# A graph convolution whose copied columns are collected over pairs of turns

## The chip, the cores and the metric

The kernel runs on one core of a Trainium2 chip. The metric is device time in microseconds (us) of one execution: the median of three runs of the kernel before is 3968.41 us, from 3967.84 to 3970.65.

## The reference

6250 nodes with 128 features and 206,250 edges sorted by destination (100,000 in both directions, and one loop per node). Two layers run one after the other, each as `x = x + layer(relu(layernorm(x)))`. The first is an attention layer with three edge types. The second, the only one that the change touches, is a convolution:

```
filters = silu(edge_attr @ fW1 + fb1) @ fW2 + fb2          # 50 attributes an edge
messages = (x[src] @ dW + db) * filters
aggregated = segment_sum(messages, dst)
return x + silu(aggregated @ uW1 + ub1) @ uW2 + ub2
```

## The kernel before

The first half of the time is the attention layer; at its end the product `x @ dW + db` of every node lies in a table in HBM (`table1`, a row per node), and the features themselves, transposed to one column per node, are read from `features` into SBUF (`by_node`, line 1561, a plane of `sums`).

**Units and turns.** The convolution goes through the edges in 269 units of 768 edges, six chunks of 128 (`CH`). Six units make a turn (`SL`); there are 45 turns (`TURNS`), the last of five units. Six gather buffers `xg[:, s]` belong to the six slots of a turn. The engines run their own instruction streams and meet at semaphores:

- GpSimd (POOL), `gather_units_beside`: for each unit one indirect DMA per chunk (line 63), which fetches 128 rows of `table1` into `xg`. A buffer is free when the product of the unit six back is done (`xg_free` is `s_msg`).
- TensorE (PE), `turn`: the first filter layer of a unit (line 1690, into `ps_h`), the second one of the unit before (line 1659, two banks `ps_f`), the sums by destination of the unit three back (line 1668), and once a turn a tile's update (1687, 1654).
- ScalarE (ACT): Silu of `ps_h` into `hid` (line 1609), and the transfers of the edge attributes (1592).
- VectorE (DVE), `turn` and `messages`: merge of a sum (line 1791), one-hot rows (1735), the bias sum on the filters (1773), then what `aside` puts in, then the product of filters and gathered rows (1783), which counts `s_msg` up. Reading the bases of a turn's windows into registers (`bases`, line 508) stands at the head of each turn.
- SyncE (SP), `load_beside`: index lists, finished tiles, and 64 rows a turn of one chunk by single row transfers (`Rows`).

**Columns.** Not every chunk is gathered. In turns 2 to 44 the last chunk of slots 1, 3 and 4 (of slot 4 half; the other half is SP's) is made from features in SBUF: VectorE and ScalarE each copy a share of the columns of its source nodes from `by_node` into `held`, one small copy a column (`collect`, lines 1748 and 1624, 4 bytes in each of 128 partitions); PE multiplies `held` by dW (`products`, line 1676); VectorE adds the bias and puts the rows into `xg` (`place`, line 1757). POOL leaves that chunk out. So a turn has 33 gathers. The addresses of the columns come from a list in SBUF (`columns`), read 16 at a time into registers (`READ`, `sources_at`, line 501). VectorE copies 24 columns a unit (144 a turn, 6192 in all), ScalarE 32, 32, 24, 32, 32, 24 (176 a turn, 7568 in all). In VectorE's order the copies stand behind the bias sum and the placement, ahead of the product.

**Loops.** VectorE's loop runs over turns 2 to 43 (`column_turns`), ScalarE's over 3 to 43 (`hinted_finishing_turns`), both with a hint for the branch back; PE's (`finishing_turns`) and POOL's have none. The turns ahead of a loop are written out.

Of the kernel before, what the change touches and what calls it, by code (L numbers as in the profile page):

```python
# [24 lines left out]
P = 128  # L25
CH = 6
UE = CH * P
SL = 6
NU = -(-E // (UE * SL)) * SL
TURNS = NU // SL  # L30
# [500 lines left out]
def hinted_finishing_turns(nc, engine, body):  # L531

    body(0, True, SL)
    for i in range(1, OPEN + 1):
        body(i, False, SL)
    with nc.Fori(OPEN + 1, SHUT, engines=[engine], hint_back_edge=True) as i:
        body(i, False, SL)
    body(SHUT, False, REST)


# [17 lines left out]
class Column:  # L558


    def __init__(self, to, placed, late, vector, scalar):
        self.to, self.placed, self.late, self.vector, self.scalar = to, placed, late, vector, scalar
        self.count = vector + scalar
# [3 lines left out]
COLUMNS = (Column(1, 5, False, 58, 70), Column(3, 1, True, 57, 71), Column(CARRY_SLOT, 3, True, 29, 35))  # L567
COLUMN_TURNS = TURNS - 2
TO = [column.to for column in COLUMNS]
ROWS = 64  # L570
ROW_TURNS = TURNS - 3
STORES = 48


class Share:


    def __init__(self, counts, held):
        self.counts, self.total = counts, sum(counts)
        self.held = [(m, e) for m, es in enumerate(held) for e in es]  # L580
        self.first, self.last = ({m: es[k] for m, es in enumerate(held)} for k in (0, -1))
        assert self.total == len(self.held)

    def start(self, s):
        return sum(self.counts[:s])

    def slot(self, s):
        return self.held[self.start(s):self.start(s + 1)]
# [6 lines left out]
def collects(i):  # L595
    return not (isinstance(i, int) and not 1 <= i <= COLUMN_TURNS)


def places(i, column):
    first = 2 if column.late else 1  # L600
    return not (isinstance(i, int) and not first <= i < first + COLUMN_TURNS)


def takes(i):
    return not (isinstance(i, int) and i < 2)


def column_rows(rows):

    turn = np.arange(2, TURNS)  # L610
    chunk = [rows[(turn * SL + to) * CH + CH - 1] for to in TO]
    return np.concatenate([chunk[m][:, e:e + 1] for share in (SCALAR, VECTOR) for m, e in share.held], 1)
# [7 lines left out]
def column_at(r, i, m):  # L620

    return r * COLUMN_TURNS * len(COLUMNS) + (i - 1) * len(COLUMNS) + m
# [27 lines left out]
def landed_beside(r, i, s):  # L650

    if s in TO:
# [5 lines left out]
def column_turns(nc, engine, body):  # L658

    body(0, True, SL)  # L660
    body(1, False, SL)
    with nc.Fori(2, TURNS - 1, engines=[engine], hint_back_edge=True) as i:
        body(i, False, SL)
    body(TURNS - 1, False, REST)
# [153 lines left out]
def gather_units_beside(pool, passes, table, xg, idx, idx_in, gathered, xg_free, pool_turn):  # L818

    with pool.Fori(0, passes) as r:  # L820
        def turn(i, first, count):
            for s in range(count):
                if s % LOAD == 0:
                    pool.wait_ge(idx_in[s // LOAD], 16 * (r * TURNS + i + 1))
                pool.wait_ge(xg_free, r * UNITS + (XS if first else i * SL + s + 1))  # L825
                pool.sem_inc(pool_turn, 1)
                for c in range(CH - 1 if s in TO and takes(i) else chunks_of(i, s)):
                    k = s % LOAD * CH + c
                    gather(pool, xg[:, s, c, :], table, idx[s // LOAD][:, k:k + 1], gathered[s])

        turn(0, True, SL)
        turn(1, False, SL)
        with pool.Fori(2, TURNS - 1) as i:
            turn(i, False, SL)
        turn(TURNS - 1, False, REST)


class Rows:
# [9 lines left out]
    def landed(self, eng, r, i, s):  # L848
        if s == CARRY_SLOT and takes(i) and not (isinstance(i, int) and i == TURNS - 1):
# [13 lines left out]
def load_beside(nc, sp, a, h, idx, idx_in, gathered, landed, rows, xg, xg_free, ahead, beside, listed):  # L863

    def read(r, i, v, count=SL):

        s = min(v * LOAD + LOAD, count) - 1
        sp.wait_ge(gathered[s], landed_beside(r, i, s))
# [635 lines left out]
def convolution_edges(nc, h, a, acc, update, table, features, planes, sent, sources, project, y, out):  # L1504

    with ExitStack() as ctx:
# [23 lines left out]
        drawn = sb("drawn", [COLUMN_TURNS, SCALAR.total + VECTOR.total], i32)  # L1530
        columns = sb("columns", [33, COLUMN_TURNS * SCALAR.total], i32)
        by_row = [drawn[:, 0:SCALAR.total], drawn[:, SCALAR.total:]]
        held = sb("held", [P, len(COLUMNS), P])
# [10 lines left out]
        def _(sp):  # L1544
# [6 lines left out]
            sp.dma_start(drawn[:, :], a["column_rows"][:, :]).then_inc(lists_in, 16)  # L1551

            sp.wait_ge(scaled, 2)
            for k, share in enumerate((SCALAR, VECTOR)):
                sp.dma_start(columns[32 * k:32 * k + 1, 0:COLUMN_TURNS * share.total].rearrange("o (t c) -> o t c", c=share.total), by_row[k]).then_inc(table_in, 16)

            def tables(r):

                sp.wait_ge(project.last_turned, 16)
                sp.wait_ge(s_column, r * COLUMN_TURNS * len(COLUMNS) + len(COLUMNS))  # L1560
# [25 lines left out]
        def _(act):  # L1586
            act.wait_ge(w_in, 64)
            act.wait_ge(update.loaded, 64)
            with act.Fori(0, pass_count(act, h)) as r:
# [5 lines left out]
                def turn(i, first, count):  # L1595
                    for s in range(count):
# [6 lines left out]
                        if opens(i) and s == 1:  # L1603
                            k = r * DONE + i - OPEN
                            act.wait_ge(t_u, k + 1)
                            if not (isinstance(i, int) and i == OPEN):
                                act.wait_ge(t_v, k)
# [3 lines left out]
                        if collects(i):  # L1611
                            collect(i, s)

                def collect(i, s):

                    if s == 0:
                        act.wait_ge(table_in, 16 * (r + 3))
                        act.sem_inc(begun, 1)
                    starts = sources_at(nc, mybir.EngineType.Activation, columns[0:1, :], (i - 1) * SCALAR.total + SCALAR.start(s), SCALAR.counts[s])
                    for (m, k), start in zip(SCALAR.slot(s), starts):  # L1620
                        if k == SCALAR.first[m]:
                            act.wait_ge(s_column, column_at(r, i, m) + 1)
                            act.sem_inc(begun, 1)
                        one = nc.scalar.copy(held_bytes[:, 4 * (m * P + k):4 * (m * P + k) + 4], by_byte[:, bass.ds(start, 4)])  # L1624
                        if k == SCALAR.last[m]:
                            one.then_inc(s_other, 1)
                hinted_finishing_turns(nc, mybir.EngineType.Activation, turn)
# [10 lines left out]
        def _(pe):  # L1638
# [4 lines left out]
            with pe.Fori(0, pass_count(pe, h)) as r:  # L1643
                def filters(n, s, fresh, i=None, at=None):
# [10 lines left out]
                    for m, column in enumerate(COLUMNS):  # L1655
                        if at is not None and at[1] == column.placed and places(at[0], column):
                            products(at[0] - 1 if column.late else at[0], m, b)
# [13 lines left out]
                def products(i, m, b):  # L1671

                    k = column_at(r, i, m)
                    pe.wait_ge(s_half, k + 1)
                    pe.wait_ge(s_other, k + 1)
# [238 lines left out]
```

## Time and profile before

| | |
|---|---|
| runs, median (lowest to highest) | 3968.41 us (3967.84 to 3970.65) |
| profiled execution, its own time | 3967.15 us |
| its span, first to last instruction | 3965.3 us |
| mean granted TensorE clock | 0.624 |
| gathers of the convolution (line 63) | 1485, 947 ns each, busy 1406.5 us |
| column copies on ScalarE (line 1624) | 7568, busy 796.0 us, idle before them 325.4 us |
| column copies on VectorE (line 1748) | 6192, busy 688.5 us, idle before them 258.9 us |
| message products on VectorE (line 1783) | 269, 957 ns each, idle before them 151.2 us |

A group's busy time is the time in which at least one of its instructions ran; idle is the time in which its engine stood still just ahead of them, with what ended most of it. "issue" means that the profile shows nothing it waited for: the engine's sequencer was reading registers, computing addresses or fetching. DVE is VectorE, ACT ScalarE, POOL GpSimd, SP SyncE; a q behind the name is its sequencer or queue. Granted clock 1.0 is 2.4 GHz, 0.5 is 1.2 GHz.

### The profile page before, as it was taken

The page shows a single profiled execution, that of the slowest core. Times are in us where ns is not written, and L with a number is a line of the kernel's source. Part 1 is how long each engine was busy: PE and PEld are TensorE (multiplying, and loading weights), DVE is VectorE, ACT ScalarE, POOL GpSimd, SP SyncE. Part 2 cuts the span into 40 slices and gives each one's busy share as a digit, 9 for nine tenths or more (in the row PEclk, how much of TensorE's full clock was granted, in tenths as well). Part 3 has the DMA queues.
Part 4 walks back from the last instruction along what each step waited for, and adds up shares of the span by engine and source line. Part 5 has one row for each costly group of instructions (what it writes and reads, how often), then busy time and mean ns, then how long its engine had stood idle before and what let it go on. Part 6 is the DMA issues. An engine that isn't in the chain of part 4 may idle for free. (4 is left out here: it accounts for less than half of the span.)

```text
span 3965.3 us, 95687 instructions
## 1 busy us (share of the span) xinstructions
PE 3326.2 (84%) x14263; PEld 2589.5 (65%) x14264; DVE 3095.7 (78%) x11649; ACT 2162.5 (55%) x10967; POOL 2948.0 (74%) x3109
## 2 busy tenths in 40 slices
PE   5788888888888888888876898889888889999898
PEld 3566666666666666666655776767676767777676
DVE  7888888888888888888875777777777777777775
ACT  5455555555555555555543665556555565655563
POOL 6777777777777777777757777777777777777776
PEclk7555555555555555555557777777777777767767
DMA  4222222222222222222225332333233332333232
GB/s 127 57 62 61 62 64 62 62 63 63 63 61 63 62 63 62 62 63 63 60 48 145 83 81 76 80 81 79 77 80 80 81 80 76 81 80 81 75 81 68
DMA packets 193989, 289.07 MB, mean 73 GB/s; under 512 B 85379, under 2 KB 138047, under 8 KB 189036
## 3 DMA queue, kind: packets, MB, share of 16 engines
q0 software_dynamic: 98464, 205.11, 21.8%
q1 hardware_dynamic: 90364, 40.65, 4.1%
q10 hardware_dynamic: 4840, 40.55, 3.4%
q14 instruction: 306, 2.51, 0.2%
q8 instruction: 15, 0.25, 0.0%
HBM read 267.39 MB, written 15.70 MB: 71 GB/s over the span
## 5 line engine op out<-in xcount | busy, mean ns | idle before, releaser
L63 POOL DMA_INDIRECT ae_xg<-table,ae_idx x1592 | 1502.3, 944 | 491.6 <-issue 487.4
L63 POOL DMA_INDIRECT ce_xg<-table,ce_idx x1485 | 1406.5, 947 | 458.8 <-issue 443.6
L1624 ACT COPY ce_held<-sums 128x4 uint8 x7568 | 796.0, 189 | 325.4 <-issue 311.3
L1748 DVE COPY ce_held<-sums 128x4 uint8 x6192 | 688.5, 199 | 258.9 <-issue 243.0
L1150 PE MATMUL ae_ps_k<-ae_xg,ae_e 128*96 128x129 f32 x3224 | 880.8, 431 | 0.0
L1150 PEld LDWEIGHTS ae_ps_k<-ae_xg,ae_e 128*96 128x96 f32 x3224 | 688.6, 276 | 126.5 <-issue 117.0
L1659 PE MATMUL ce_ring<-ce_fw,ce_hid 128*128 128x128 f32 x3228 | 610.2, 362 | 61.1 <-DVE ce_msg L1783 60.8
L1659 PEld LDWEIGHTS ce_ring<-ce_fw,ce_hid 128*128 128x128 f32 x3228 | 564.6, 269 | 138.5 <-DVE ce_msg L1783 90.7
L1690 PE MATMUL ce_ps_h<-ce_ea,ce_fw 50*128 50x384 f32 x1076 | 532.9, 626 | 45.8 <-DMA ce_ea<-in_edge_attr 29.2
L1062 ACT ACTIVATE ae_upper<-ring 128x576 f32<-128x576 f32 x269 | 174.9, 650 | 671.5 <-DVE ring L1327 671.5
L1668 PEld LDWEIGHTS ce_ring<-ce_hot,ce_msg 128*128 128x128 f32 x3224 | 487.0, 236 | 5.2 <-DVE ce_msg L1783 5.2
L1609 ACT ACTIVATE ce_hid<-ce_ps_h,ce_fb 128x768 f32<-128x768 f32 x269 | 241.8, 899 | 445.9 <-issue 279.0
L1668 PE MATMUL ce_ring<-ce_hot,ce_msg 128*128 128x32 f32 x3224 | 476.1, 305 | 2.8 <-DVE sums L1791 2.8
L1070 ACT ACTIVATE ae_off<-cst,plan 128x96 bf16<-128x96 f32 x1614 | 454.1, 363 | 5.0 <-DVE plan L491 5.0
L1783 DVE TENSOR_TENSOR ce_msg<-ce_ring,ce_xg 128x768 f32<-128x768 f32 x269 | 257.5, 957 | 151.2 <-DMA ce_xg<-table,ce_idx 146.1
L1198 PE MATMUL ring<-ae_rise,cst 64*128 64x192 f32 x538 | 270.2, 604 | 83.4 <-DVE ae_rise L1350 80.4
L1165 PE MATMUL ae_ps_tz<-cst,ae_high 128*96 128x128 f32 x269 | 120.2, 447 | 255.1 <-DVE ae_high L1337 255.1
L1690 PEld LDWEIGHTS ce_ps_h<-ce_ea,ce_fw 50*128 50x128 f32 x1076 | 219.4, 226 | 167.5 <-issue 65.7
L1327 DVE TENSOR_TENSOR ring<-ring,ae_xg 128x576 f32<-128x576 f32 x269 | 205.9, 766 | 129.7 <-DMA ae_xg<-table,ae_idx 126.0
L1337 DVE TENSOR_REDUCE ae_high<-ae_e 128x96 f32<-128x576 f32 x269 | 304.6, 1132 | 0.0
L1773 DVE TENSOR_TENSOR ce_ring<-ce_ring,ce_fb 128x768 f32<-128x768 f32 x269 | 257.7, 958 | 58.1 <-PE ce_ring L1659 57.9
L1165 PEld LDWEIGHTS ae_ps_tz<-cst,ae_high 128*96 128x96 f32 x269 | 41.8, 156 | 319.6 <-DVE ae_high L1337 319.6
(193 smaller groups left out, 3804.8 us busy)
## 6 DMA issues: line engine op xcount, KB each, us to landing
ce_stage<-table SPq DMA_DIRECT2D x2688, 0.5 KB
ae_stage<-table SPq DMA_DIRECT2D x2560, 0.5 KB
ce_ea<-in_edge_attr ACTq DMA_DIRECT2D x88, 450.0 KB
ae_xg<-table,ae_idx POOLq DMA_INDIRECT x1592
ce_xg<-table,ce_idx POOLq DMA_INDIRECT x1485
sums<-in_x SPq DMA_DIRECT2D x7, 448.0 KB, 4.5
sums<-features SPq DMA_DIRECT2D x1, 3136.0 KB
table<-sums SPq DMA_DIRECT2D x6, 462.0 KB, 3.6
```

The source lines that it names most:

```text
L63: eng.indirect_dma_start(out=out, out_offset=None, in_=table[:, :], in_offset=bass.IndirectOffsetOnAxis(ap=idx, axis=0)).then_inc(done, 16)
L1070: last = nc.scalar.activation(off[:, s % 2, c, :], h.iota, ACT.Square, bias=keys[:, c:c + 1], scale=STEP)
L1150: last = nc.tensor.matmul(ps_k[0:KEYS, 0:D + 1], by_chunk[s % 3][:, c, :], xg[:, s % XS, c, 0:D + 1], start=(c == 0), stop=(c == count - 1))
L1198: nc.tensor.matmul(ps_m[s % 2][:, 0:2 * KEYS], h.raised_by[0:64, :], rise[:, :, :].rearrange("p a k -> p (a k)"), start=True, stop=True).t ...
L1337: nc.vector.tensor_reduce(out=high[:, :], in_=by_chunk[s % 3].rearrange("p c k -> p k c"), op=ALU.max, axis=AX.X).then_inc(s_high, 1)
L1624: one = nc.scalar.copy(held_bytes[:, 4 * (m * P + k):4 * (m * P + k) + 4], by_byte[:, bass.ds(start, 4)])
L1659: last = nc.tensor.matmul(ps_f[b][:, c * D:(c + 1) * D], hid[:, b, c * P:(c + 1) * P], fw2[:, :], start=True, stop=True)
L1668: last = nc.tensor.matmul(ps_a[s % 2][:, 0:W], msg[:, s % 3, c, :], hot[:, s % 3, c, :], start=(c == 0), stop=(c == count - 1))
L1690: last = nc.tensor.matmul(ps_h[:, k * 512:k * 512 + H], fw1[:, :], ea[:, s // LOAD, q:q + H], start=True, stop=True)
L1748: one = nc.vector.tensor_copy(held_bytes[:, 4 * (m * P + k):4 * (m * P + k) + 4], by_byte[:, bass.ds(start, 4)])
L1773: nc.vector.tensor_tensor(filt, filt, fb2[:, :].unsqueeze(1).to_broadcast([P, CH, D]), ALU.add).then_inc(s_bias, 1)
L1783: nc.vector.tensor_tensor(msg[:, s % 3, :, :], filt, xg[:, s % XS, :, :], ALU.mult).then_inc(s_msg, 1)
```

## The change

All convolution loops run over pairs of turns: pair k is turns 2k+1 and 2k+2, k from 0 to 21; pairs 1 to 20 are the loop, the rest is written out. VectorE's and ScalarE's loops keep the hint and get a set position of their first instruction (`head_slot` 8 and 100). A pair collects seven chunks in its twelve units. Each engine copies 32 columns a unit, half of every chunk: 384 a pair, 8224 in all (the last pair collects three chunks, in five units). The seventh chunk is the last one of slot 0 of the odd turns 3 to 43; POOL leaves it out too. `held` has four buffers in place of three, used in rotation. The lists are laid out by pair and reach SBUF by way of `msg`; VectorE and ScalarE wait for them ahead of their loops. A column is placed three units after its last copies. In VectorE's order nothing else moves.

```diff
-COLUMNS = (Column(1, 5, False, 58, 70), Column(3, 1, True, 57, 71), Column(CARRY_SLOT, 3, True, 29, 35))
-COLUMN_TURNS = TURNS - 2
+PAIRS = TURNS // 2
+PIECE, HELD = 32, 4
+COLUMNS = (Column(1, 1, (0, 1), P), Column(3, 1, (2, 3), P), Column(CARRY_SLOT, 1, (4,), P - ROWS), Column(0, 2, (5, 6), P),
+           Column(1, 2, (7, 8), P), Column(3, 2, (9, 10), P), Column(CARRY_SLOT, 2, (11,), P - ROWS))
...
+        self.to, self.ahead, self.slots, self.count = to, ahead, slots, count
+        self.late, self.placed = divmod(slots[-1] + 3, 2 * SL)
...
-SCALAR = Share([32, 32, 24] * 2, [range(c.vector, c.count) for c in COLUMNS])
-VECTOR = Share([24] * SL, [range(c.vector) for c in COLUMNS])
...
+def since(m):
+    return HELD if m >= HELD else len(COLUMNS) - (m + HELD if m + HELD < len(COLUMNS) else m) + m
...
+def served(i, k, p, s):
+    if isinstance(i, int) and i < 2 + (s == 0):
+        return None
+    return next(((m, column.ahead - 1) for m, column in enumerate(COLUMNS) if column.to == s and column.ahead == 2 - p), None)
...
+def paired_turns(pairs, body):
+    body(0, True, SL, None, 0)
+    for i in (1, 2):
+        body(i, False, SL, 0, i - 1)
+    with pairs as k:
+        for p in range(2):
+            body(2 * k + 1 + p, False, SL, k, p)
+    body(TURNS - 2, False, SL, PAIRS - 1, 0)
+    body(TURNS - 1, False, REST, PAIRS - 1, 1)
+
+def hinted_pairs(nc, engine, slot):
+    return nc.Fori(1, PAIRS - 1, engines=[engine], hint_back_edge=True, head_slot={engine: slot})
...
-                for c in range(CH - 1 if s in TO and takes(i) else chunks_of(i, s)):
+                for c in range(chunks_of(i, s) if served(i, k, p, s) is None else CH - 1):
...
+            dve.wait_ge(lists_in, 64)
...
-                    if s == 0:
-                        dve.wait_ge(table_in, 16 * (r + 3))
-                        dve.sem_inc(begun, 1)
-                    starts = sources_at(nc, mybir.EngineType.DVE, columns[32:33, :], (i - 1) * VECTOR.total + VECTOR.start(s), VECTOR.counts[s])
-                    for (m, k), start in zip(VECTOR.slot(s), starts):
-                        if k == VECTOR.first[m]:
-                            dve.wait_ge(s_column, column_at(r, i, m) + 1)
-                            dve.sem_inc(begun, 1)
-                        one = nc.vector.tensor_copy(held_bytes[:, 4 * (m * P + k):4 * (m * P + k) + 4], by_byte[:, bass.ds(start, 4)])
-                        if k == VECTOR.last[m]:
-                            one.then_inc(s_half, 1)
+                    m, first = column_in(q)
+                    if not COLUMNS[m].here(k):
+                        return
+                    if q == COLUMNS[m].slots[0]:
+                        dve.wait_ge(s_column, column_at(r, k, m) + 1 + len(COLUMNS) - since(m))
+                        dve.sem_inc(begun, 1)
+                    if q == 0:
+                        dve.wait_ge(table_in, 16 * (r + 1))
+                        dve.sem_inc(begun, 1)
+                    at = 4 * (m % HELD * P + 0 * COLUMNS[m].count // 2 + first)
+                    starts = sources_at(nc, mybir.EngineType.DVE, columns[0:1, :], k * pair_columns + q * PIECE, PIECE)
+                    for start in starts:
+                        last = nc.vector.tensor_copy(held_bytes[:, at:at + 4], by_byte[:, bass.ds(start, 4)])
+                        at += 4
+                    if q == COLUMNS[m].slots[-1]:
+                        last.then_inc(s_half, 1)
...
-                hinted_finishing_turns(nc, mybir.EngineType.Activation, turn)
+                paired_turns(hinted_pairs(nc, mybir.EngineType.Activation, 100), turn)
...
-                column_turns(nc, mybir.EngineType.DVE, turn)
+                paired_turns(hinted_pairs(nc, mybir.EngineType.DVE, 8), turn)
```

## Rows read from the trace of the kernel before

**Rows 1.** The page, part 1: each engine's busy us, share, instructions.
```profile
PE 3326.2 (84%) x14263; PEld 2589.5 (65%) x14264; DVE 3095.7 (78%) x11649; ACT 2162.5 (55%) x10967; POOL 2948.0 (74%) x3109
```

**Rows 2.** Windows: busy us by engine, granted clock, DMA share, GB/s.
```profile
2222.00:3915.00 1693.00, 1512.21 (x7301) 1206.28 (x7300) 1234.48 (x7094) 986.22 (x7476) 1280.46 (x1354) 0.74 0.31 79
```

**Rows 3.** The chain of waits of that stretch, shares by line.
```profile
by line: POOL ce_xg L63 56.1%; issue 22.0%; DMA ce_xg<-table,ce_idx 4.9%; PE ce_ring L1659 3.4%; PE ce_ps_h L1690 3.1%; PE ce_ring L1668 2.3%; DVE ce_held L1748 1.3%; DVEq L501 1.0%; DVE ce_msg L1783 0.8%; POOLq L825 0.6%; DMA ce_idx<-in_sr
```

**Rows 4.** POOL's group in that stretch: busy, mean ns, idle, releasers.
```profile
L63 POOL DMA_INDIRECT ce_xg<-table,ce_idx x1354 | 1281.3, 946 | 412.8 <-issue 404.9 <-DVE ce_msg L1783 6.7 <-DMA ce_idx<-in_src 1.2
```

**Rows 5.** VectorE's waits in that stretch: us in total, times, longest us.
```profile
DVE ce_msg L1783 <- DMA ce_xg<-table,ce_idx: 124.6, 69, 3.9
...
DVE ce_ring L1773 <- PE ce_ring L1659: 30.9, 27, 2.4
DVE ce_done L1811 <- DMA out_x<-ce_done: 4.1, 8, 0.8
```

**Rows 6.** VectorE's timeline, two turns: start, us, instruction, idle before.
```profile
2184.80 0.96 DVE L1783 TENSOR_TENSOR ce_msg<-ce_ring,ce_xg 128x768 f32<-128x768 f32 x1
2186.28 0.19 DVE L1791 TENSOR_TENSOR sums<-sums,ce_ring 128x32 f32 x1 [0.53 <-issue]
...
2194.08 0.28 DVE L1757 TENSOR_TENSOR ce_xg<-ce_ring,pj_parts 128x128 f32<-128x128 f32 x1
2194.27 1.71 DVE L1748 COPY ce_held<-sums 128x4 uint8 x16
2196.65 0.92 DVE L1748 COPY ce_held<-sums 128x4 uint8 x8 [0.67 <-issue]
...
2221.80 0.96 DVE L1783 TENSOR_TENSOR ce_msg<-ce_ring,ce_xg 128x768 f32<-128x768 f32 x1
...
3007.67 0.19 DVE L1791 TENSOR_TENSOR sums<-sums,ce_ring 128x32 f32 x1 [0.74 <-issue]
...
3009.62 1.89 DVE L1748 COPY ce_held<-sums 128x4 uint8 x16 [0.56 <-issue]
```

**Rows 7.** Two lines on VectorE: count, ns min/median/max.
```profile
L501 DVEq TENSOR_LOAD <-ce_columns x516: 594/852/1126, 2148.8 to 3912.5; - x172
...
L1748 DVEq ALU_OP  x5904: 40/40/45, 2226.0 to 3913.8; - x197
L1748 DVE COPY ce_held<-sums x5904: 150/172/431, 2226.1 to 3913.9; 128x4 uint8 x197
```

**Rows 8.** ScalarE: its timeline, and its largest wait in the stretch.
```profile
3003.17 0.90 ACT L1609 ACTIVATE ce_hid<-ce_ps_h,ce_fb 128x768 f32<-128x768 f32 x1 [3.32 <-issue]
...
3009.44 0.89 ACT L1609 ACTIVATE ce_hid<-ce_ps_h,ce_fb 128x768 f32<-128x768 f32 x1
...
3012.96 1.80 ACT L1624 COPY ce_held<-sums 128x4 uint8 x16 [0.92 <-issue]
...
3019.84 0.76 ACT L1624 COPY ce_held<-sums 128x4 uint8 x7 [0.48 <-issue]
...
ACT ce_hid L1609 <- issue: 272.5, 95, 5.2
```

**Rows 9.** PE's timeline at 1.2 GHz, filters to filters.
```profile
2859.64 2.93 PE L1659 MATMUL ce_ring<-ce_fw,ce_hid 128*128 128x128 f32 x12
...
2868.34 1.06 PE L1659 MATMUL ce_ring<-ce_fw,ce_hid 128*128 128x128 f32 x4
```

**Rows 10.** The head: VectorE's timeline, its first bias sum.
```profile
2123.05 0.97 DVE L1773 TENSOR_TENSOR ce_ring<-ce_ring,ce_fb 128x768 f32<-128x768 f32 x1 [9.37 <-PE ce_ring L1659]
```

**Rows 11.** VectorE's timeline: products at the ends of three stretches.
```profile
2143.45 0.96 DVE L1783 TENSOR_TENSOR ce_msg<-ce_ring,ce_xg 128x768 f32<-128x768 f32 x1 [3.26 <-DMA ce_xg<-table,ce_idx]
...
3876.23 0.96 DVE L1783 TENSOR_TENSOR ce_msg<-ce_ring,ce_xg 128x768 f32<-128x768 f32 x1
...
3914.81 0.96 DVE L1783 TENSOR_TENSOR ce_msg<-ce_ring,ce_xg 128x768 f32<-128x768 f32 x1 [0.70 <-DMA ce_xg<-table,ce_idx]
...
3953.55 0.96 DVE L1783 TENSOR_TENSOR ce_msg<-ce_ring,ce_xg 128x768 f32<-128x768 f32 x1 [4.77 <-DMA ce_xg<-table,ce_idx]
```

More of the change, by code:

```diff
@@ L528, in finishing_turns @@
     body(SHUT, False, REST)
[L531 to L538, printed above, removed]
 def opens(i):
@@ L558, with __init__, pair, here @@
 class Column:
-    def __init__(self, to, placed, late, vector, scalar):
-        self.to, self.placed, self.late, self.vector, self.scalar = to, placed, late, vector, scalar
-        self.count = vector + scalar
+    def __init__(self, to, ahead, slots, count):
+        self.to, self.ahead, self.slots, self.count = to, ahead, slots, count
+        self.late, self.placed = divmod(slots[-1] + 3, 2 * SL)
+    def pair(self, k):
+        return k - self.late
+    def here(self, k):
+        return not (isinstance(k, int) and not 0 <= k < (PAIRS if self.ahead == 1 else PAIRS - 1))
@@ L572 @@
 STORES = 48
[L575 to L588, printed above, removed]
-SCALAR = Share([32, 32, 24] * 2, [range(c.vector, c.count) for c in COLUMNS])
@@ L592, with column_in @@
-VECTOR = Share([24] * SL, [range(c.vector) for c in COLUMNS])
[L595 to L605, printed above, removed]
-def column_rows(rows):
-    turn = np.arange(2, TURNS)
-    chunk = [rows[(turn * SL + to) * CH + CH - 1] for to in TO]
-    return np.concatenate([chunk[m][:, e:e + 1] for share in (SCALAR, VECTOR) for m, e in share.held], 1)
+def column_in(q):
+    return next((m, PIECE * column.slots.index(q)) for m, column in enumerate(COLUMNS) if q in column.slots)
@@ new lines, in since @@
+def since(m):
[4 more added lines that the diff above has]
+    return next(((m, column.ahead - 1) for m, column in enumerate(COLUMNS) if column.to == s and column.ahead == 2 - p), None)
+def column_rows(rows):
+    pair = np.arange(PAIRS)
+    padded = np.concatenate([rows, np.zeros((SL * CH, P), rows.dtype)])
+    chunk = [padded[((2 * pair + 1 + column.ahead) * SL + column.to) * CH + CH - 1] for column in COLUMNS]
+    parts = []
+    for half in range(2):
+        for q in range(2 * SL):
+            m, e = column_in(q)
+            first = half * COLUMNS[m].count // 2 + e
+            parts.append(chunk[m][:, first:first + PIECE])
+    return np.concatenate(parts, 1)
@@ L820, in gather_units_beside, with turn @@
     with pool.Fori(0, passes) as r:
-        def turn(i, first, count):
+        def turn(i, first, count, k, p):
             for s in range(count):
@@ L826, in turn @@
                 pool.sem_inc(pool_turn, 1)
-                for c in range(CH - 1 if s in TO and takes(i) else chunks_of(i, s)):
[L828 to L835, printed above, removed]
+                for c in range(chunks_of(i, s) if served(i, k, p, s) is None else CH - 1):
+                    j = s % LOAD * CH + c
+                    gather(pool, xg[:, s, c, :], table, idx[s // LOAD][:, j:j + 1], gathered[s])
+        paired_turns(pool.Fori(1, PAIRS - 1), turn)
 class Rows:
@@ L848, in landed @@
     def landed(self, eng, r, i, s):
-        if s == CARRY_SLOT and takes(i) and not (isinstance(i, int) and i == TURNS - 1):
+        if s == CARRY_SLOT and not (isinstance(i, int) and (i < 2 or i == TURNS - 1)):
             eng.wait_ge(self.carried, 16 * (r * ROW_TURNS + i - 1))
@@ L1655, in filters @@
                     for m, column in enumerate(COLUMNS):
-                        if at is not None and at[1] == column.placed and places(at[0], column):
-                            products(at[0] - 1 if column.late else at[0], m, b)
+                        if at is not None and at[0] is not None and at[1] == column.placed and column.here(column.pair(at[0])):
+                            products(column.pair(at[0]), m, b)
                     for c in range(CH):
@@ L1762, in aside @@
                         return
-                    i, s = at
+                    k, q = at
                     for m, column in enumerate(COLUMNS):
-                        if s == column.placed and places(i, column):
-                            place(i - 1 if column.late else i, m, (s - 1) % SL % 2)
-                    if collects(i):
-                        collect(i, s)
-                def messages(n, s, i, at=None):
+                        if q == column.placed and column.here(column.pair(k)):
+                            place(column.pair(k), m, (q - 1) % SL % 2)
```

131 lines of the change are left out of this document (68 added, 63 removed).

## The prediction

> **What bounds the kernel now.** I began with the page's busy shares [rows 1]. They single out no engine: PE is busy for 84%, VectorE (DVE) for 78%, GpSimd (POOL) for 74%. The change touches only the second half, the convolution, so I cut out its steady stretch, 2222 to 3915 us, in which VectorE goes 41 times round its loop: 1693.0 / 41 = 41.29 us a turn [rows 2]. The chain of waits of that stretch is POOL's gather for 56.1%, with 22.0% "issue" [rows 3]. POOL's group says what that issue is: its gathers are busy for 1281.3 us with 412.8 idle between them, of which 404.9 wait for nothing, the step from one gather to the next [rows 4]. So (1281.3 + 412.8) / 1354 = 1.251 us a gather, 33 a turn, 41.29 us: POOL alone sets the turn.
>
> Next comes how much air the others have. VectorE's waits for other engines and transfers in the stretch are 124.6 + 30.9 + 4.1 [rows 5] and 3.9 in two smaller groups, 163.5 us, 3.99 a turn. The rest of its turn, 37.30 us, is its own: instructions, and "issue" gaps in which its sequencer reads sources into registers or computes addresses. A turn early in the stretch, when POOL is still ahead, confirms it: from one message product at 2184.80 to the one six units on at 2221.80 there are 37.0 us, without an outside wait [rows 6]. So the slack under POOL is 4.0 us a turn, and the question is what the change adds to VectorE.
>
> **POOL's part.** Per pair of turns one more chunk (slot 0 of the odd turn) comes from the table in SBUF, 21 gathers fewer in all: 65 a pair, or 81.3 us, 40.66 a turn. If POOL stays the bound this is worth 21 x 1.251 = 26.3 us. That is all the change can gain there.
>
> **VectorE's part.** It copied 144 columns a turn (24 a unit: a read of 16 registers and 16 copies, a read of 8 and 8 copies). Now it copies 32 a unit, 192 a turn: the second read is of 16 too, with 16 copies behind it.
> - Copies: a batch of 8 spans 0.92 us and one of 16 spans 1.71 us [rows 6], so 8 more cost 0.79; by batches that start on an idle engine (1.89 less 0.92 [rows 6]) 0.97. With 0.17 for one copy [rows 7], (0.92 - 0.17) / 7 = 0.107 us a copy. I take 0.86 us a unit, 5.14 a turn.
> - Register reads: half are of 16 and half of 8, so minimum and maximum are the two sizes: 0.594 and 1.126 us, the median 0.852 lying between the halves [rows 7]. I take 1.10 for the long one. The second read is bare: between the 16 and the 8 copies the engine idles 0.66 us each time [rows 6]. ScalarE, which has both sizes, idles 0.48 us ahead of 8 copies and 0.92 ahead of 16 [rows 8]. So the gap grows by 0.44 (ScalarE) to 0.53 us; I take 0.50 a unit, 3.0 a turn. The first read lies under the bias sum (0.96 us) before as after.
> - Placements: 7 a pair in place of 6, at 0.28 us [rows 6] and two waits: 0.2 a turn. Waits and semaphore steps at a column's start: 3.5 a turn instead of 3, but at a unit's head, not between copies: 0.
>
> Sum: 5.14 + 3.0 + 0.2 = 8.3 us a turn against a slack of 4.0. Nothing covers it: copies, reads, bias sum, product and merge are one engine's one queue. VectorE's turn becomes 37.3 + 8.3 = 45.6 us (45.3 from the 37.0), above POOL's 40.66. I take 45.5. Below, the cheapest reading is 36.5 + 0.79 x 6 + 0.44 x 6 = 43.9 (36.5 estimated as 37.0 less the 0.5 us before the merge [rows 6]); above, it is 37.3 + 0.97 x 6 + 0.53 x 6 + 0.3 = 46.6.
>
> **ScalarE's part.** 176 columns a turn become 192, two of its six units growing from 24 to 32. A unit of 32 takes from 3009.44 to 3014.76, 5.3 us [rows 8], six of them 32, and the stall at its loop's back edge (3.32 us [rows 8]), now once a pair, 1.7 more. The issue of two attribute transfers and one small activation a turn would have to cost 11 us before ScalarE reached 45.5: no cost. The fourth held buffer and `since` make each collection wait for the product four columns back, placed at least one slot earlier in PE's order: no cost.
>
> **PE's part.** Half a product more a turn (0.5 to 0.8 us). At a clock of 1.2 GHz a unit takes 8.70 us (2859.64 to 2868.34) [rows 9]; over the stretch PE is busy for 1512.2 / 246 = 6.15 us a unit, at a granted clock of 0.74, so about half of the time at each level [rows 2]. A unit will be 7.58 us on VectorE, so PE falls behind 1.1 us a unit while slow and catches up when fast. It can: filters are two banks deep, so they can be ready some 4.6 us (7.6 less 2.93) before VectorE wants them. With less slack (6.88 a unit) it made VectorE wait 30.9 us in 1693 [rows 5]. I add nothing.
>
> **The head.** VectorE now waits, before it builds the keys, for the two transfers of the column lists, which SP issues as soon as they are scaled. I estimate up to 5 us for them, half of what follows: behind the keys VectorE idles 9.37 us for the first filters (2123.05) [rows 10]. Cost 0, at most 3. The lists in `msg` are dead before the first product.
>
> **The tail.** Turn 44 copies nothing. Before, POOL holds it: 3914.81 to 3953.55, 38.7 us [rows 11]. Now POOL has these gathers nearly done when VectorE arrives, and the six units run at PE's pace, 6.15 each: 36.9, a gain of 1.8 (from 0 to 10). Turn 43 has five units of 32 columns and one of none: 45.5 less 4.7 (twice 1.71, and 1.2 for the read and the gap between), 40.8 against 38.6 (3876.23 to 3914.81), +2.2.
>
> **The sum**, on the profiled run's own 3967.15 us (its span is 3965.3): the copies' stretch runs from 2143.45 to 3876.23 [rows 11], 42 turns and 1732.8 us. Its first turn (41.3 us) has 4 us of start-up waits that stay: 41.3 + 8.3 = 49.6. The other 41 x 45.5 = 1865.5. Together 1915.1, +182.3; with tail and turn 43, +182.7. The changed kernel takes 3967.15 + 182.7 = **4150 us**; the median of the runs, 3968.41, is 1.3 above the profiled run, too little to move it.
>
> **A rule against the change: the back edge.** VectorE goes round its loop almost free: ahead of the first merge of a turn it idles 0.53 us in a turn that stands outside the loop (2186.28) and 0.74 where it has just gone round (3007.67) [rows 6]. ScalarE, with a slightly longer body, stands 3.32 us "issue" at each turn's head, and over the stretch its activations have 272.5 us of such idle [rows 8]. A body of a pair has on VectorE more than twice the instructions. If VectorE then stalls as ScalarE does, that is 20 times 3.3 us = 66 us. The Trainium skill (Runtime: NRT & Kernel Launch, section "Instruction fetch mechanics") gives the reason: an engine holds two pages of 256 instructions, and a branch back to a page it no longer holds waits for a fetch. By that rule a body over 512 instructions cannot stay, and the new one has 768 in its copies alone, an address and a copy for each column; whether the prefetch hint and the new head slots (8 and 100) hide the fetch, no trace here shows.
>
> **Rivals.**
> - VectorE stalls at the back edge: 4150 + 66 = 4216 us. For: ScalarE's stall with the same hint. Against: VectorE's own back edge, hinted too, costs 0.2 us [rows 6]. 14%.
> - POOL stays the bound and the change is faster: VectorE's new work would have to fit in 4.0 us a turn. It decides where the addition falls below 4.0: over half of the 8.3 would have to vanish. 3967 - 26 = 3941 us. 5%.
> - The longer reads and their gap cost nothing (hidden behind queued copies): 37.3 + 5.3 = 42.6 a turn, 41 x 42.6 + 46.6 = 1793, +60: 4028 us. Against it the bare 0.66. 6%.
> - PE's slow phases are not absorbed: half the units at 8.7 and half at 7.6 give 48.9 us a turn, 41 x 3.4 more: 4150 + 139 = 4289 us. For: the waits for filters. Against: the two banks. 6%.
> - My forecast, VectorE the bound at 45.5 us: 69%, own range 4100 to 4185.
>
> **Numbers.** Range 4090 to 4230: it holds the forecast with its bounds and the back edge, and leaves out 4028, 3941 and 4289 (17%) with a little of the tails. A measurement of this kernel can tell 0.2% (8 us) from no change. Faster 5%; the same 2% (slack and addition happening to cancel with POOL's gain); slower 93%.
>
> **What would show it.** Right: the changed profile has VectorE's message products every 7.5 us, copies in 16 + 16 with a gap near 1.15 us, 8224 copies on each engine, hardly a wait of VectorE for gathers, and new gaps on POOL, released by VectorE's product, of some 4.8 us a turn. Long register reads and no short ones. PE's granted clock falls little. Wrong: POOL's gathers still without a break (then my price of copies or reads is wrong), gaps over 2 us on VectorE once a pair (back edge), or VectorE's wait for filters above 2 us a turn.

## The result: 4.7% slower, and the profile after

The changed kernel takes 4158.09 us (median of 4 runs, 4153.78 to 4160.27), the kernel before 3969.53 on the same chip (4 runs). The ratio is 1.0473 (95% interval 1.0455 to 1.0491), +188.6 us; the forecast was 4150. The profiled run after took 4160.1 us with a span of 4158.3.

First the page's busy shares (the row that answers to [rows 1]).

```profile
PE 3471.5 (83%) x14305; PEld 2730.8 (66%) x14306; DVE 3316.9 (80%) x13702; ACT 2208.0 (53%) x11623; POOL 2926.0 (70%) x3088
```

VectorE (DVE) has 221 us more work, 2053 instructions more; POOL has 21 instructions and 22 us less. Now the second half's steady stretch, 2327 to 4074 us, 19 rounds of the new loop (each a pair of turns), as windows; the second row is the tail.

```profile
2327.00:4074.00 1747.00, 1528.56 (x6803) 1240.19 (x6802) 1344.91 (x8418) 958.90 (x7562) 1173.28 (x1243) 0.68 0.27 71
4074.00:4158.00 84.00, 76.95 (x366) 59.85 (x365) 48.25 (x223) 23.77 (x145) 36.36 (x39) 0.74 0.20 50
```

1747.0 / 38 = 45.97 us a turn, 91.95 a pair, where [rows 2] gave 41.29 a turn. The granted clock of TensorE is 0.68 against 0.74. What now sets the turn is read from two views of that stretch: the chain of waits by line,

```profile
by line: issue 26.4%; DVE ce_held L1755 24.9%; DVEq L501 21.5%; DVE ce_ring L1780 6.4%; PE ce_ring L1662 2.8%; DVEq L508 2.3%; DVE ce_hot L1738 2.1%; PE ce_ps_h L1692 2.1%; PE ce_ring L1671 1.9%; DVEq L1755 1.4%; DVE sums L1797 1.3%; DVE ce
```

and the waits (us in total, times, longest):

```profile
POOL ce_xg L63 <- issue: 355.8, 1116, 2.4
DVE ce_held L1755 <- issue: 333.8, 377, 1.3
...
POOL ce_xg L63 <- DVE ce_msg L1789: 218.2, 127, 3.3
...
DVE sums L1797 <- issue: 38.9, 38, 1.8
...
DVE ce_msg L1789 <- issue: 9.4, 19, 0.5
...
DVE ce_hot L1738 <- issue: 6.0, 19, 0.3
DVE ce_ring L1780 <- PE ce_ring L1662: 1.3, 4, 0.4
```

POOL's gather, 56.1% of the chain in [rows 3], is gone from it. VectorE's copies (L1755) and its sequencer's reads of their sources (L501) stand in its place. VectorE waited 163.5 us for others before [rows 5]; now the last row is the only one of that kind, 1.3 us. POOL waits instead, for VectorE's message product, 218.2 us, 5.7 a turn where I had said some 4.8. The timeline of VectorE shows one pair's beginning, with start, duration (us), instruction and the idle time before it:

```profile
3064.02 0.96 DVE L1789 TENSOR_TENSOR ce_msg<-ce_ring,ce_xg 128x768 f32<-128x768 f32 x1
3066.70 0.19 DVE L1797 TENSOR_TENSOR sums<-sums,ce_ring 128x32 f32 x1 [1.72 <-issue]
...
3068.60 1.93 DVE L1755 COPY ce_held<-sums 128x4 uint8 x16 [0.52 <-issue]
3071.53 1.77 DVE L1755 COPY ce_held<-sums 128x4 uint8 x16 [1.00 <-issue]
3073.30 0.96 DVE L1789 TENSOR_TENSOR ce_msg<-ce_ring,ce_xg 128x768 f32<-128x768 f32 x1
...
3078.88 1.77 DVE L1755 COPY ce_held<-sums 128x4 uint8 x16 [1.12 <-issue]
3080.76 0.96 DVE L1789 TENSOR_TENSOR ce_msg<-ce_ring,ce_xg 128x768 f32<-128x768 f32 x1
```

Where [rows 6] had 16 + 8 copies with 0.66 us between, there are 16 + 16 with 1.00 to 1.12. The line of the reads, and the copies' group of the page (each of the two engines makes 8224):

```profile
L501 DVEq TENSOR_LOAD <-ce_columns x514: 1095/1101/1305, 2151.5 to 4110.3; - x172
...
L1755 DVE COPY ce_held<-sums 128x4 uint8 x8224 | 909.9, 202 | 379.5 <-issue 376.7
```

No short read is left (minimum 594 ns in [rows 7]). The ends of the stretches, as VectorE's products (they answer to [rows 11]):

```profile
2147.59 0.96 DVE L1789 TENSOR_TENSOR ce_msg<-ce_ring,ce_xg 128x768 f32<-128x768 f32 x1
...
4073.79 0.96 DVE L1789 TENSOR_TENSOR ce_msg<-ce_ring,ce_xg 128x768 f32<-128x768 f32 x1
...
4113.35 0.96 DVE L1789 TENSOR_TENSOR ce_msg<-ce_ring,ce_xg 128x768 f32<-128x768 f32 x1
```

| stretch (us) | before | forecast | after |
|---|---|---|---|
| 42 turns with copies | 1732.8 | 1915.1 | 1926.2 |
| turn 43 | 38.6 | 40.8 | 39.6 |
| last turn and what follows it (to the span's end) | 50.5 | 48.7 | 44.9 |
| up to the first of these products | 2143.4 | 2143.4 | 2147.6 |

The differences are +193.4, +1.0, -5.5 and +4.1: 193.0, as the spans have it (4158.3 less 3965.3).

### The profile page after: what moved, and what is told of

The parts are those of the page before. It is cut to its first block and busy times, and to the rows that moved or that the text cites. A ratio compares the mean times of both kernels' runs of the same rounds, so it can differ in the third digit from the quotient of the medians.

```text
span 4158.3 us, 100937 instructions
## 1 busy us (share of the span) xinstructions
PE 3471.5 (83%) x14305; PEld 2730.8 (66%) x14306; DVE 3316.9 (80%) x13702; ACT 2208.0 (53%) x11623; POOL 2926.0 (70%) x3088
## 5 line engine op out<-in xcount | busy, mean ns | idle before, releaser
L63 POOL DMA_INDIRECT ce_xg<-table,ce_idx x1464 | 1384.4, 946 | 653.4 <-issue 419.8
L1755 DVE COPY ce_held<-sums 128x4 uint8 x8224 | 909.9, 202 | 379.5 <-issue 376.7
L1625 ACT COPY ce_held<-sums 128x4 uint8 x8224 | 841.7, 189 | 376.7 <-issue 359.1
L1145 PEld LDWEIGHTS ae_ps_k<-ae_xg,ae_e 128*96 128x96 f32 x3224 | 688.7, 277 | 126.4 <-issue 117.0
L1662 PE MATMUL ce_ring<-ce_fw,ce_hid 128*128 128x128 f32 x3228 | 685.3, 394 | 81.6 <-DVE ce_msg L1789 81.1
L1662 PEld LDWEIGHTS ce_ring<-ce_fw,ce_hid 128*128 128x128 f32 x3228 | 637.3, 299 | 164.0 <-DVE ce_msg L1789 125.0
L1692 PE MATMUL ce_ps_h<-ce_ea,ce_fw 50*128 50x384 f32 x1076 | 541.9, 635 | 27.7 <-DMA ce_ea<-in_edge_attr 24.5
L1671 PEld LDWEIGHTS ce_ring<-ce_hot,ce_msg 128*128 128x128 f32 x3224 | 536.3, 256 | 1.0 <-issue 0.7
L1671 PE MATMUL ce_ring<-ce_hot,ce_msg 128*128 128x32 f32 x3224 | 519.9, 321 | 0.0
L1160 PEld LDWEIGHTS ae_ps_tz<-cst,ae_high 128*96 128x96 f32 x269 | 41.9, 156 | 318.1 <-DVE ae_high L1332 318.1
```

What stands on the lines that cost most here:

```text
L63: eng.indirect_dma_start(out=out, out_offset=None, in_=table[:, :], in_offset=bass.IndirectOffsetOnAxis(ap=idx, axis=0)).then_inc(done, 16)
L1145: last = nc.tensor.matmul(ps_k[0:KEYS, 0:D + 1], by_chunk[s % 3][:, c, :], xg[:, s % XS, c, 0:D + 1], start=(c == 0), stop=(c == count - 1))
L1625: last = nc.scalar.copy(held_bytes[:, at:at + 4], by_byte[:, bass.ds(start, 4)])
L1662: last = nc.tensor.matmul(ps_f[b][:, c * D:(c + 1) * D], hid[:, b, c * P:(c + 1) * P], fw2[:, :], start=True, stop=True)
L1671: last = nc.tensor.matmul(ps_a[s % 2][:, 0:W], msg[:, s % 3, c, :], hot[:, s % 3, c, :], start=(c == 0), stop=(c == count - 1))
L1692: last = nc.tensor.matmul(ps_h[:, j * 512:j * 512 + H], fw1[:, :], ea[:, s // LOAD, q:q + H], start=True, stop=True)
```

## Experiments

The theory is the forecast's: VectorE's own queue sets the turn, and of what the change added 5.1 us a turn is copies and 3.0 is the longer bare read. The rivals are a stall at the pair loop's back edge, a POOL that stays the bound, and PE's slow phases. Each edit is against the changed kernel; ratios are against the kernel before, run on the same chip.

**Parts of the added work taken away from VectorE.** In e1 and e8 its second read is of 8 registers, in e2 it makes 24 copies, in e3 both. None of the four computes the whole convolution: in e1 and e8 most columns in the second half of a piece of 32 come from a wrong source, in e2 and e3 eight of 32 stay zero.

```diff
 # e1_reads_24: read 24 sources, copy 32; the last 8 sources serve two copies each
-starts = sources_at(..., k * pair_columns + q * PIECE, PIECE)
-for start in starts:
+starts = sources_at(..., k * pair_columns + q * PIECE, 24)
+for start in twice(starts):        # from the 17th on each source twice
```

> VectorE reads 16 + 8 addresses a unit and still makes 32 copies (its last 8 copies take an address a second time). VectorE bound with bare reads: 0.50 us a unit less, 3.0 of 45.9 a turn, 42 turns, 126 us off the changed kernel's 4158: 4032 us. If the longer reads hide behind queued copies: 4158 us, no change.

3948.74 us (3945.0 to 3960.77), ratio 0.996 (0.9926 to 0.9994): 83 us below what was expected. VectorE's timeline tells why.

```profile
3064.13 1.72 DVE L1763 COPY ce_held<-sums 128x4 uint8 x16
3066.51 1.23 DVE L1763 COPY ce_held<-sums 128x4 uint8 x16 [0.66 <-issue]
```

The second batch of 16 spans 1.23 us, not 1.77. By the line's rows there are 6168 address computations for 8224 copies:

```profile
L1763 DVE COPY ce_held<-sums x8224: 150/172/429, 2147.8 to 3896.4; 128x4 uint8 x196
L1763 DVEq ALU_OP  x6168: 40/40/47, 2147.8 to 3896.1; - x199
```

Two copies from the same source share one computation, so the edit took away eight of these per unit as well, and POOL was the bound again (it waited 2.7 us for VectorE's products in 1500). The mended twin has distinct sources:

```diff
 # e8_reads_24_distinct, in twice()
-            yield start
+            yield start + 4
```

> As e1, but each of VectorE's 32 copies has an address computation of its own again (the last 8 take an address read before, plus 4 bytes, so these columns are another node's). If e1 gained twice because copies that share an address skip that computation (0.071 us instead of 0.107, 16 of them a unit, 3.3 us a turn) and the shorter read gave 3.0: now only the read's part remains, 4158 - 126 = 4032 us. If the read alone gave e1's whole gain: 3949 us again.

4032.08 us (4029.34 to 4034.82), ratio 1.0159 (1.0139 to 1.0179). As expected: with 8224 computations the batch is back at 1.77 us, behind the same short gap.

```profile
L1763 DVEq ALU_OP  x8224: 40/40/47, 2150.9 to 3986.5; - x196
```

```profile
3070.70 1.77 DVE L1763 COPY ce_held<-sums 128x4 uint8 x16 [0.66 <-issue]
```

The eight registers more per read are worth 4158.1 - 4032.1 = 126 us, 126 / 42 = 3.0 us a turn, the term as priced. Next the copies, and both.

```diff
 # e2_copies_24: 32 sources read, the last 8 not copied (held is zeroed once, ahead)
 for e, start in enumerate(starts):
+    if e >= 24:
+        continue
 # e3_both_24: 24 read, 24 copied
```

> VectorE reads all 32 addresses a unit and copies only the first 24 (8 columns of each piece stay zero). VectorE bound at 0.107 us a copy: 5.1 us a turn less, 40.8, beside POOL's 40.7: 3950 to 3980 us. If VectorE's copies were not what sets the turn (PE's slow phases or ScalarE instead): above 4100 us.

> VectorE reads 24 addresses and copies 24 (the other 8 columns of each piece stay zero), all else as in the changed kernel. VectorE falls to 37.9 us a turn, POOL with its 21 gathers fewer is the bound again at 40.66: 3935 to 3955 us, 26 below the kernel before. If POOL's saved gathers are worth nothing (another engine as late as POOL): 3968 or more.

e2: 3940.81 us (3938.87 to 3946.94), ratio 0.9935 (0.9912 to 0.9957), 9 us below the range expected. e3: 3941.67 (3941.03 to 3942.75), 0.9934 (0.9911 to 0.9956). Both are where POOL would be the bound (3941). In e3, between 2400 and 3900 us, POOL's waits are

```profile
POOL ce_xg L63 <- issue: 360.9, 1184, 0.3
POOL ce_xg L63 <- DVE ce_msg L1790: 4.3, 14, 0.3
```

so its gathers run without a break, 1.25 us each, 65 a pair. Two things follow: the form with pairs costs nothing by itself and brings the gain of 21 fewer gathers (27 us, 26.3 worked out); and what eats them is VectorE's work. In e2 the long gap stays (3076.77, ahead of 8 copies), and still the time is POOL's: without the copies VectorE's turn is at most POOL's 40.7, so by the turn the copies were worth at least 45.97 - 40.7 = 5.3 us. Their own busy time gives the size. The rows are one batch of e2 and e2's group of copies over the whole run:

```profile
3076.77 0.92 DVE L1758 COPY ce_held<-sums 128x4 uint8 x8 [1.07 <-issue]
```

```profile
L1758 DVE COPY ce_held<-sums 128x4 uint8 x6168 | 688.7, 200 | 395.3 <-issue 391.3
```

The changed kernel's group has 909.9 us (above), both in 257 units: (909.9 - 688.7) / 257 = 0.86 us a unit, 5.2 a turn, where 5.14 was forecast.

**The back edge.**

```diff
 # e4_no_hint: VectorE's loop alone loses the hint of its branch
-hint_back_edge=True
+hint_back_edge=engine != mybir.EngineType.DVE
```

> VectorE's loop without the hint for its branch back, its position kept. If the hint is what keeps the fetch of the loop's first block out of the way: some 3.3 us a pair more, 20 pairs, 4158 + 66 = 4224 us. If the block is fetched in time anyway: 4158 us; if every pair pays already, no change either.

4194.52 us (4193.83 to 4195.21), ratio 1.0566 (1.0536 to 1.0597): 36 us above the changed kernel. Once a pair, ahead of the merge of its first turn, VectorE idles 4.04 us in place of 1.72:

```profile
3087.66 0.19 DVE L1797 TENSOR_TENSOR sums<-sums,ce_ring 128x32 f32 x1 [4.04 <-issue]
```

In the waits of 2400 to 3900 us the merge's idle is this without the hint, and this in the changed kernel:

```profile
DVE sums L1797 <- issue: 69.4, 32, 4.2
```

```profile
DVE sums L1797 <- issue: 34.4, 33, 1.7
```

So the stall exists and the hint covers it here; unhinted it is 4.04 - 1.72 = 2.3 us a pair by the timeline, (69.4 - 34.4) / 16.3 pairs = 2.1 by the waits, not the 3.3 that the rival took from ScalarE. The run's own 36 us, 1.8 a pair, are about half of the 66 expected.

**Six chunks a pair in place of seven**: the added chunk, and so two units' copies, dropped; POOL gathers it again (41.3 us a turn).

```diff
 # e5_six_chunks (and what column_in() and landed_beside() need for it)
-COLUMNS = (..., Column(CARRY_SLOT, 1, (4,), P - ROWS), Column(0, 2, (5, 6), P),
+COLUMNS = (..., Column(CARRY_SLOT, 1, (4,), P - ROWS),
 # e9_six_chunks: e5, and held buffers given so that no collection waits for a late product
+BUFFER, SINCE = (0, 1, 2, 3, 1, 2), (6, 3, 3, 6, 3, 3)
```

> Loops over pairs, but without the seventh chunk (slot 0 of the odd turn is gathered again; slots 5 and 6 of a pair collect nothing): 320 columns a pair on each engine. VectorE bound theory: VectorE falls by 64 x 0.17 = 11 us a pair to 81.1, POOL sets 82.6 as before: 3968 to 3990 us. If the form of the loop (longer body, instruction fetch, one common pace of the engines) is what costs: above 4050 us.

4112.44 us (4095.67 to 4116.63), ratio 1.0349 (1.0324 to 1.0374), a miss by over 120. ScalarE idled up to 10.2 us ahead of its copies, which I took for waits for a held buffer, so I mended the buffers:

> As e5, with the buffers of held given out so that no collection waits for a product that PE issues only in the next pair. If e5's time was that new wait (ScalarE stood 8 us a pair in it), it goes and VectorE's own 84 us a pair is the bound: 3975 to 4000 us. If the form of the loop costs: 4110 us again.

4125.99 us (4120.35 to 4145.25), ratio 1.0412 (1.0384 to 1.0439): a second miss. The longest idle ahead of ScalarE's copies is down to 1.1 us and the time no better, so that wait was not the cause. VectorE's timeline in e9, over the two units that now copy nothing:

```profile
3064.66 0.96 DVE L1789 TENSOR_TENSOR ce_msg<-ce_ring,ce_xg 128x768 f32<-128x768 f32 x1
...
3067.14 0.96 DVE L1789 TENSOR_TENSOR ce_msg<-ce_ring,ce_xg 128x768 f32<-128x768 f32 x1 [0.29 <-DVE ce_ring L1780]
...
3070.35 0.96 DVE L1789 TENSOR_TENSOR ce_msg<-ce_ring,ce_xg 128x768 f32<-128x768 f32 x1
...
3078.52 0.97 DVE L1780 TENSOR_TENSOR ce_ring<-ce_ring,ce_fb 128x768 f32<-128x768 f32 x1 [6.26 <-PE ce_ring L1662]
```

These units take 2.5 and 3.2 us, then VectorE stands 6.26 us for the next filters. PE's timeline shows why they are late:

```profile
3056.34 1.61 PE L1662 MATMUL ce_ring<-ce_fw,ce_hid 128*128 128x128 f32 x12 [1.53 <-DVE ce_msg L1789]
...
3065.89 0.77 PE L1678 MATMUL ce_ring<-pj_dw,ce_held 128*128 128x128 f32 x2 [5.20 <-DVE ce_msg L1789]
3066.45 2.77 PE L1662 MATMUL ce_ring<-ce_fw,ce_hid 128*128 128x128 f32 x12
```

PE had stood 5.20 us until VectorE's product gave it a bank, and the twelve matmuls of the filters took 2.77 us behind that wait where they took 1.61 before it. It needs 6.15 us a unit on the mean [rows 2] and 8.70 at 1.2 GHz [rows 9] and is at most two banks ahead, so a mean over the pair says nothing: VectorE cannot save up what the empty units leave. The waits for filters are 95.8 us in 1500, 1.3 in the changed kernel; over the 1900 us of the turns with copies that is some 120 us, the size of the miss.

Both times lie where "the form of the loop costs" would have put them. That reading is out by e3, which has the same form and loses nothing, and by the idle ahead of the merges in e9, 34.9 us in 1500 where the changed kernel has 34.4. No run here has more than two banks, so that a third would help is not shown.

**Columns moved from VectorE to ScalarE**, with the whole result. 28 to 36:

```diff
 # e6_28_36 (each engine's list at its own stride, the small lists moved to a third row)
-PIECE, HELD = 32, 4
+PIECES_OF, HELD = (28, 36), 4
 # e7_28_36_bases: e6, and VectorE reads the bases of 12 units once a pair, not 6 twice
+elif p == 0: base = pair_bases[:] = bases(..., i * SL - back, 2 * SL)
 # e10_28_36_at104: e6, and the loop's head at another slot
-paired_turns(hinted_pairs(nc, mybir.EngineType.DVE, 8), turn)
+paired_turns(hinted_pairs(nc, mybir.EngineType.DVE, 104), turn)
```

> The changed kernel with its columns shared out anew: VectorE 28 a unit, ScalarE 36; all seven chunks, the reference's whole output. VectorE bound theory: 4 x 0.17 us a unit less on VectorE, 41.9 us a turn, ScalarE at some 41: 4158 - 172 = 3986 us, up to 4010 where the two get in each other's way. If total copying and not VectorE's share sets the turn: 4100 us or more.

> As the one before, and the bases of both turns of a pair are read by VectorE in one read of 12 registers at the pair's head instead of two of 6. VectorE bound theory: the gap ahead of a merge goes once a pair, some 0.5 us a turn if VectorE is still the bound: 20 us below the one before, about 3970. If ScalarE or POOL is the bound there: no change from it.

> As e6, with the first instruction of VectorE's loop at position 104 in place of 8, so that the branch back stands where it stands in the changed kernel (104 + 893 = 997 = 8 + 989). If the 2.2 us that e6 stands at each back edge come from that position: 1.7 us a pair less, 4037 - 35 = 4002 us. If they come from the body's length or its contents: 4037 us.

e6: 4036.57 us (4029.81 to 4058.65), ratio 1.0158 (1.0141 to 1.0175), 27 us above the range expected. e7: 4046.81 (4042.62 to 4051.0), 1.0198 (1.0181 to 1.0215), a miss: it was to gain 20 and lost 10. e10: 4017.01 (3988.58 to 4021.47), 1.0097 (1.006 to 1.0134), the best that computes everything, and still behind the kernel before; it is 20 us below e6 where 35 were expected (37 by the two profiled runs, 4058.65 and 4021.47). The merge's idle tells them apart, in the waits of 2400 to 3900 us of e6, of e7 and of e10:

```profile
DVE sums L1797 <- issue: 68.4, 34, 3.9
```

```profile
DVE sums L1799 <- issue: 92.9, 18, 5.6
```

```profile
PE ce_ps_h L1692 <- ACT ce_hid L1606: 63.2, 47, 3.6
...
DVE sums L1797 <- issue: 32.3, 33, 1.8
...
DVE ce_ring L1780 <- PE ce_ring L1662: 12.6, 16, 1.2
...
DVE sums L1797 <- PE ce_ring L1671: 3.5, 2, 1.8
```

Taking copies out of VectorE's loop made its body shorter, and with the head at the same slot the branch came to lie elsewhere: the stall returned in full although the hint stood (68.4 against 34.4; unhinted 69.4). Four copies fewer in 12 units, each a copy and an address computation, are 96 instructions; moving the head by 96 slots puts the branch back to where the changed kernel has it, and took the stall away: 32.3. e1 bears this out: its loop is shorter by 96 address computations with the head at slot 8, so by this count its branch lies where e6's does, though it has all 32 copies. Its merges' idle in the same stretch, hidden there under POOL, is

```profile
DVE sums L1805 <- issue: 65.2, 33, 3.8
```

e8, with these computations back, has 36.4.

In e7 the long read of the bases stands bare right behind that stall. The rows are the read of 6 bases at the head of a pair in the changed kernel, and e7's read of 12:

```profile
L508 DVEq TENSOR_LOAD <-base_i x1: 1422/1422/1422, 3064.9 to 3064.9; - x1
```

```profile
L508 DVEq TENSOR_LOAD <-base_i x1: 2742/2742/2742, 3014.4 to 3014.4; - x1
```

That is 1.3 us more a pair, against the 0.33 us of idle ahead of the second turn's merge that it saves.

VectorE is still the bound in e10: it waits 12.6 + 3.5 us for PE in 1500, and its 212 bias sums in that stretch make 42.5 us a turn, above POOL's 40.66. The 41.9 expected of VectorE's own turn held (42.5 less 0.5 of waits). PE's 63.2 us for ScalarE's hidden layer reach VectorE only as far as those 16 us.

27 to 37:

```diff
 # e11_27_37: as e10
+PIECES_OF, HELD = (27, 37), 4
 # e12_27_37_aligned: every unit's list begins at a multiple of 16 bytes
+PIECES_OF, STRIDES, HELD = (27, 37), (28, 40), 4
```

> As e10, with 27 columns a unit on VectorE and 37 on ScalarE. VectorE bound theory: 12 x 0.17 = 2 us a pair less on VectorE, 82.2, with ScalarE and POOL beside it at 81 to 82: 3955 to 3985 us. If ScalarE is already the bound at 36: slower than e10.

5105.5 us (5102.55 to 5107.77), ratio 1.2861 (1.2839 to 1.2882): a miss by over 1100. The line of the reads, on both engines of e11:

```profile
L501 ACTq TENSOR_LOAD <-ce_columns x771: 549/1229/3674, 2147.9 to 5058.7; - x193
L501 DVEq TENSOR_LOAD <-ce_columns x514: 1110/2515/3732, 2150.3 to 5054.2; - x172
```

A read takes up to 3.7 us, three times that of [rows 7]. With pieces of 27 and 37 words the lists of three units in four begin off a multiple of 16 bytes. The test pads them:

> As e11 (27 columns a unit on VectorE, 37 on ScalarE), with each unit's list at a stride of 28 and 40 words in place of 27 and 37, so that every read starts at a multiple of 16 bytes. In e11 only every fourth unit's list starts so, and VectorE's reads took 1.1 us there and 3.6 us in the units between. If the place of the list in SBUF is the cause, all reads fall to 1.1 us and the kernel to 3975 to 4010 us, VectorE at 81.7 us a pair with ScalarE as late. If the odd numbers of reads or copies are the cause: 5105 us again.

4079.47 us (4071.08 to 4083.93; before 3977.28 on that chip), ratio 1.0253 (1.0239 to 1.0267), 69 us above the range expected. The reads of e12 and, below, of e10:

```profile
L501 ACTq TENSOR_LOAD <-ce_columns x771: 541/1013/1232, 2153.4 to 4030.2; - x193
L501 DVEq TENSOR_LOAD <-ce_columns x514: 1102/1204/1356, 2154.9 to 4033.6; - x172
```

```profile
L501 DVEq TENSOR_LOAD <-ce_columns x514: 845/984/1164, 2148.2 to 3966.8; - x172
```

The place of the list is the cause of e11's loss: padding alone took away 1026 us. But e12 is still 62 us behind e10 (54 against the kernel before on each chip), though e10 copies one column a unit more on VectorE. The median of e12's reads, of 16 and 11 registers, is 1204 ns where that of e10's, of 16 and 12, is 984, and the idle ahead of copies in 1500 us is 344.6 against 277.1, 67 us more. One read of 11, alone in its window:

```profile
L501 DVEq TENSOR_LOAD <-ce_columns x1: 1294/1294/1294, 3003.5 to 3003.5; - x1
```

A read of 11 takes longer than one of 12 (0.85 us, the minimum in e10) or of 16 (1.11, the one before it). The durations on record fit two prices. Aligned reads of 8, 12 and 16 take 0.594, 0.85 and 1.10 us, some 0.07 a register. Reads that begin off a multiple of 16 bytes take some 0.23 a register: 16 in 3.65 us (e11), 12 in 2.74 (e7), 6 in 1.42 (the bases at the head of a pair, whose list there begins at word 12k + 2). And 11 is 8 at the low price and 3 at the high one: 0.594 + 3 x 0.23 = 1.28. The 6 bases of a pair's second turn, whose list begins at word 12k + 8, would be 4 and 2 in the same way; they take 0.82. This is worked out from the traces after the runs; no run was made to test it.

## Why the prediction was right, step by step

- **POOL bounds before; slack 4.0 us a turn.** Held: with VectorE's load taken back (e3) the time is POOL's, 3941.67 against 3941 worked out. Those 26 us were real, and lost.
- **Copies, 5.14 us a turn.** Held: 5.2 by the busy time of the copies in the changed kernel and in e2, and a batch of 16 spans 1.77 us where I took 1.71. By the measured turn e2 gives only a bound, at least 5.3, which also holds what else VectorE's turn had beyond the forecast.
- **Longer bare read, 3.0 us a turn.** Measured 3.0 (e8). The idle ahead of copies is 333.8 / 38 = 8.8 us a turn, where it was 232.0 / 41 = 5.7 in the stretch of [rows 2]. The rival "reads hidden" put its no-cost case at 4028; taking the cost away gave 4032, so the size was right and the rival wrong.
- **VectorE's turn 45.5.** 45.97; I missed 0.47. The idle ahead of merges is what it was, 38.9 / 38 = 1.0 us a turn; new are the short ones ahead of a product and of a one-hot, once a pair each, (9.4 + 6.0) / 38 = 0.4. 38 x 0.47 = 18 us too little; against it the four turns ahead of the loop's steady part took 179.4 us (2147.59 to 2327.0), 44.9 each, where I had 49.6 + 3 x 45.5 = 186.1. Net +11 of the 1915.1: two errors of opposite sign, so that 4150 came closer to 4158 than the turn alone would have brought it.
- **ScalarE, PE no cost.** Held. PE's rival needed waits of VectorE for filters; they fell from 30.9 us [rows 5] to 1.3, though the granted clock fell from 0.74 to 0.68. The two banks cover slow phases as long as each unit is long (7.66 us); e9 shows the case where they do not.
- **Head 0, tail -1.8, turn 43 +2.2.** The wait for the lists came (5.71 us, estimated up to 5) and was hidden in the idle ahead of the first bias sum, 4.52 us where it was 9.37 [rows 10], as VectorE's timeline shows:

```profile
2109.96 0.56 DVE L475 TENSOR_SCALAR ce_ring<-ubase,narrow,sweep 128x270 f32<-128x270 f32 x1 [5.71 <-issue]
...
2126.20 0.97 DVE L1780 TENSOR_TENSOR ce_ring<-ce_ring,ce_fb 128x768 f32<-128x768 f32 x1 [4.52 <-PE ce_ring L1662]
```

  That sum starts 3.2 us later than in [rows 10], but VectorE already entered the convolution later: its clearing of the sums (128x6304) starts at 2097.01 where it did at 2092.24. The last turn and what follows take 5.5 us less, inside the gain of 0 to 10, of which I took the small end. Turn 43 costs 1.0.
- **Back-edge rival, 4216.** I read the merge at 2186.28 as one outside the loop. It is the first merge of turn 2, the loop's first round, which no branch back precedes, so the comparison stands: both it and 3007.67 are in even turns. Ahead of an odd turn's merge the kernel before idles more, 1.33 us (2967.31), since its bases take 1.42 us to read and an even turn's 0.82. Of the changed kernel's 1.72 us at a pair's head, an odd turn, only 0.4 is new. The stall exists, at 2.1 to 2.3 us a pair instead of 3.3, and the hint hid it in this kernel (e4); e6, e10 and e1 show that this is a matter of where the branch lies. The Trainium skill (Runtime: NRT & Kernel Launch, section "Instruction fetch mechanics") has a taken branch wait when its target is not among the pages held. e4 agrees in kind. Neither the page nor a run here says at which places the hint fails: 34.4 and 32.3 us with the branch at one place, 68.4 and 65.2 at another.

## What to carry to other kernels

Before work moves from the engine that bounds to another, subtract: here 8.3 us a turn by the estimate, 45.97 - 37.3 = 8.7 by the measurement, went onto an engine with 4.0 of slack, to save 0.6 on the one that bounded. On an engine that copies by addresses from registers, count what the sequencer does, the read that stands bare and the address for each copy, not the copies' busy time. When a loop's body changes length, look again at the idle ahead of its first instruction; it can cost as much as the edit gives.

## What the runs showed of the hardware that I had not expected

- A copy of 128x4 bytes from a register's address takes 0.107 us in a row when each has its own address computation, and (1.23 - 0.17) / 15 = 0.071 when two share one (e1, e8). So the sequencer's address computation set the pace, not the copy; that e1 also reads each of these columns twice is a difference that no run separates.
- Reads of 16 registers from SBUF: 1.10 us (median, changed kernel). With lists that begin off a multiple of 16 bytes, up to 3.73 us; the whole kernel 1026 us slower (e11 less e12). The count matters too: 11 registers took 1.29 us and 12 took 0.85, both from aligned lists (e12, e10).
- With the hint set, the stall at a loop's branch was there or not by where the branch lay: 2 us a pair between the merges of e6 and e10 (68.4 against 32.3 us over 16 to 18 pairs), for a move of 96 slots and nothing else.
- Spare time of single units is lost across a two-bank coupling: units of 2.5 and 3.2 us were followed by a wait of 6.26 us (e9).
